# Four selective-scan layers and a routed network: new places for the matrix pieces of a step, other accumulator banks, and the head of the routed part earlier

## The reference, cut to what matters

```python
h = einsum('bhid,oi,od->bho', x, weighted_sum, weight)      # (4, 512, 256), float32
x = layernorm(h)
for _ in range(4):                                          # four layers with the same weights
    n = rmsnorm(x)
    x_in, res = split(n @ W_in, 2)                          # 256 -> 2 x 512
    u = silu(causal_conv4(x_in) + conv_b)
    dt, B, C = split(u @ W_x, [64, 80])                     # 64, 16 and 16 columns
    delta = softplus(dt @ W_dt + b_dt)
    # over the 512 positions t, for 512 channels and 16 states:
    #   h[t] = exp(delta[t] * A) * h[t-1] + delta[t] * u[t] * B[t];   y[t] = sum over states of h[t] * C[t]
    x = ((y + u * Dp) * silu(res)) @ W_out
h = h + x
z = layernorm(h)                                            # 2048 tokens of 256
e = argmax(z @ W_router)                                    # one of 4 experts for each token
y = gelu(z @ W1[e] + b1[e]) @ Wo + bo + z
out = h + layernorm(y) * gamma + beta
```

## Time and profile before

| | us |
|---|---|
| three executions | 2059.36, 2062.27, 2064.65 |
| median | 2062.27 |
| profiled execution, its own time | 2073.18 |
| profiled execution, span | 2071.5 |
| busy in the span: PE, weight loads of PE, DVE, ACT, POOL | 1850.7, 1465.2, 1564.5, 1464.7, 1538.3 |

### The profile page before, as it was taken

How to read it: one execution, slowest core, us unless ns; L and a number is a source line. 1 busy time by engine, 2 the same in 40 slices (tenths; PEclk the granted TensorE clock), 3 DMA queues, 4 the chain that set the end, 5 groups by cost and what they waited for, 6 DMA issues and landing times.

```text
span 2071.5 us, 31985 instructions
## 1 busy us (share of the span) xinstructions
PE 1850.7 (89%) x12240; PEld 1465.2 (71%) x12240; DVE 1564.5 (76%) x1703; ACT 1464.7 (71%) x2467; POOL 1538.3 (74%) x896
## 2 busy tenths in 40 slices
PE   6989899999999999999999999999898986779994
PEld 3447677777777777777777777777677775669893
DVE  1358989798989897979798988888888887752232
ACT  0268888888888888888878787878797884613231
POOL 0039898889898988888888888888989896750331
PEclk9989999999999999999999999999999998899997
DMA  7211111111111111110111111111111112152542
GB/s 248 101 51 43 52 43 61 43 62 43 62 43 62 43 61 43 48 55 34 62 41 63 41 63 42 63 41 63 42 63 41 53 52 72 62 178 85 226 144 91
DMA packets 46394, 144.27 MB, mean 70 GB/s; under 512 B 7009, under 2 KB 18529, under 8 KB 42914
## 3 DMA queue, kind: packets, MB, share of 16 engines
...
## 4 chain that ended last, share of the span: by engine, by line
PE 52%; DVE 19%; issue 12%; ACT 12%; POOL 2%; DMA 2%; SPq 0%; DVEq 0%; POOLq 0%; ACTq 0%
PE b_ps L1316 12%; DVE hid L1043 10%; PE y_all L1327 9%; ACT dub_t L694 6%; ACT hid L681 5%; DVE u L851 4%; PE bank_b L1199 3%; PE bank_a L1449 3%; PE y_all L1118 3%; PE bank_b L1214 3%; PE bank_a L1223 3%; PE b_ps L1434 2%; PE y_all L1434 2%; PE bank_a L1247 2%; PE bank_a L1214 2%
## 5 line engine op out<-in xcount | busy, mean ns | idle before, releaser
L1043 DVE TENSOR_TENSOR_SCAN hid<-hid,b_ps 128x512 f32<-128x512 f32 x1024 | 1218.3, 1210 | 243.2 <-PE b_ps L1316 222.8
L504 POOL TENSOR_TENSOR hid<-hid,c_rep 128x1024 f32<-128x1024 f32 x512 | 1210.3, 2383 | 221.5 <-DVE hid L1043 221.5
L1316 PEld LDWEIGHTS b_ps<-ident,dub_t 128*128 128x128 f32 x4096 | 488.7, 143 | 375.5 <-issue 231.1
L1316 PE MATMUL b_ps<-ident,dub_t 128*128 128x128 f32 x4096 | 634.9, 278 | 78.9 <-DVE hid L1043 74.9
L681 ACT ACTIVATE hid<-delta,neg_a 128x512 f32<-128x512 f32 x1024 | 652.7, 710 | 0.2
L1327 PE MATMUL y_all<-ident,hid 128*128 128x128 f32 x4096 | 620.6, 275 | 3.8 <-POOL hid L504 3.8
L694 ACT ACTIVATE dub_t<-du_t,b_t 128x512 f32<-128x512 f32 x768 | 490.2, 711 | 54.8 <-PE b_ps L1316 53.1
L1327 PEld LDWEIGHTS y_all<-ident,hid 128*128 128x128 f32 x4096 | 485.7, 143 | 4.8 <-POOL hid L504 4.8
L495 POOL TENSOR_SCALAR dub_t<-du_t,b_t 128x512 f32<-128x512 f32 x256 | 173.8, 707 | 0.0
L1199 PE MATMUL bank_b<-xn,w_in_sb 128*128 128x512 f32 x256 | 134.5, 612 | 15.6 <-DVE xn L838 12.5
L851 DVE SCALAR_TENSOR_TENSOR u<-bank_b,conv_w_sb,u 128x511 f32<-128x511 f32 (+2 forms) x192 | 139.4, 726 | 0.7
...
## 6 DMA issues: line engine op xcount, KB each, us to landing
c_rep<-bc_dram SPq DMA_DIRECT2D x128, 512.0 KB, 3.6
...
z_dram<-du SPq DMA_DIRECT2D x2, 1408.0 KB, 18.9
...
```

What stands on the lines that cost most here:

```text
L504: nc.gpsimd.tensor_tensor(part, part, c_rep[:, n % 2, s % GROUP, :].unsqueeze(1) .broadcast_to([P, HALF, SEQ]), ALU.mult).then_inc(hc_read ...
L1043: nc.vector.tensor_tensor_scan(hid[:, i % RING, d, :], hid[:, i % RING, d, :], b_ps[d % 2][:, :], 0.0, ALU.mult, ALU.add)\
L1316: last = nc.tensor.transpose(b_ps[d % 2][:, c * P:(c + 1) * P], dub_t[:, i % DUB, c, d * P:(d + 1) * P], ident[:, :])
```

## The change

**The tables.** Every table of places has new numbers, and is now keyed by the piece; a place with s of 16 or more lies in the next step. `squares` moves from (5, 3) to (6, 0) and from `bank_a` to `bank_b`, `b_turn` from (6, 0) to (6, 3), `spread_norm` from (8, 2) to (8, 3). The backs stand at (4, 3), (6, 0), (8, 3), (9, 0) and were at (4, 2), (5, 1), (8, 0), (8, 3); the second of them now uses `bank_a`. The taps of a block no longer stand in four slots in a row. Each piece has its own wait for its bank, where some waited for more than that.

**B turned.** `b_turn` is four full transposes, and `b_copy` reads the 16 columns out of each 128.

**ACT.** A function `between` puts copies, exponentials, logarithms and gates also in the middle of a state's four decays or four products. The four gates of a step are in two pairs within state 4, (1, 0) and (2, 3), so that four table loads stand there where two stood.

**POOL.** `POOL_B` is (4, 7, 9, 13) and was (6, 7, 10, 12); in step 15 ACT makes the products with B of all states. `times_u` and `root` move by half a state.

**Head and dispatch.** Batch 0's head stands in step 14 (states 9 to 15) and its choice early in step 15; batch 1's in states 4 to 9 of step 15; `rank(0)` and `lay_out(0)` in states 10 and 11. POOL issues the first W1 load after the half (11, 1), the eight `send_z(0)` in states 12 and 13, and the second and third W1 load in states 14 and 15.

**The tail.** The first tile follows directly on the last sums; `last_back`, `last_out` and the head of batches 2 and 3 stand among tiles 0 to 6. W1 loads 7 to 11 come before `send_z(1)`. There are 12 turns of tiles in place of 11, since tiles 10 and 21 stand alone. SP's `load_z(0)` comes ahead of a store and a load of x.

```diff
+TURNS = [tuple(range(t, min(t + 2, TILES))) for t in range(0, TILES, 2)]
+TURNS += [tuple(t + TILES for t in turn) for turn in TURNS]
+TURN_OF = {t: p for p, turn in enumerate(TURNS) for t in turn}
...
-POOL_B = (6, 7, 10, 12)
+POOL_B = (4, 7, 9, 13)
...
+            r_bank = (bank_a, bank_b, bank_a, bank_b)
+            dt_bank = (bank_a, bank_b, bank_a, bank_b)
+            back_bank = (bank_b, bank_a, bank_a, bank_a)
+            out_bank = (bank_a, bank_a)
+            x_bank = (bank_b, bank_b, bank_b, bank_b)
...
+def act_b(k):
+    return tuple(range(STATE)) if k == STEPS - 1 else ACT_B
...
+    LOAD_W1_AT = {(11, 1): 0, (14, 0): 1, (15, 0): 2}
+    SEND_Z_AT = {(12, 0): (0, 1), (12, 1): (2, 3), (13, 0): (4, 5), (13, 1): (6, 7)}
...
-                if live(k + 1) and (s, half) == (6, 1):
+                if live(k + 1) and (s, half) == (7, 0):
                     times_u(k + 1, 0)
-                if live(k + 1) and (s, half) == (7, 1):
+                if live(k + 1) and (s, half) == (8, 0):
                     times_u(k + 1, 1)
-                if live(k + 2) and (s, half) == (5, 1):
+                if live(k + 2) and (s, half) == (6, 0):
                     root(k + 2)
-                if live(k) and half == 1 and s + 3 in POOL_B:
+                if inner(k) and half == 1 and s + 3 in POOL_B:
                     times_b(k, s + 3)
-                if k == STEPS - 1 and (s, half) == (3, 0):
+                if (k, s, half) == (STEPS - 2, 11, 1):
                     head_root(0)
-                if k == STEPS - 1 and (s, half) == (10, 1):
+                if (k, s, half) == (STEPS - 1, 6, 0):
                     head_root(1)
...
+            if d == HALF:
+                between(k, s, 1)
...
+            if tc == HALF and s:
+                between(k, s - 1, 3)
...
+    def between(k, s, part):
+        at = (s, part)
+        if at == (1, 3) and live(k - 2):
+            x_copy(k - 2, 1)
+        if at == (4, 1) and live(k + 1):
+            nc.scalar.preload_act_table(ACT.Silu)
+            gate(k + 1, 1)
+            gate(k + 1, 0)
+            for m in range(NI):
+                silu(k + 1, m)
+            nc.scalar.preload_act_table_set("natural_log_exp_and_others")
+        if at == (4, 3) and live(k + 1):
+            nc.scalar.preload_act_table(ACT.Silu)
+            gate(k + 1, 2)
+            gate(k + 1, 3)
+            nc.scalar.preload_act_table_set("natural_log_exp_and_others")
...
+        if at == (7, 2) and live(k + 1):
+            delta_exp(k + 1, 0)
+            delta_log(k + 1, 0)
+        if at == (7, 4) and live(k + 1):
+            delta_exp(k + 1, 1)
+        if at == (8, 0) and live(k + 1):
+            delta_log(k + 1, 1)
...
-    TAP_AT = {(9, 2): (0, 0), (9, 3): (0, 1), (10, 0): (0, 2), (10, 1): (0, 3),
...
+    TAP_AT = {(0, 0): (9, 2), (0, 1): (10, 1), (0, 2): (10, 2), (0, 3): (10, 3),
...
-    JOIN_AT = {(1, 0): (0, 0), (2, 1): (0, 1), (9, 0): (1, 0), (9, 3): (1, 1)}
...
-                last = nc.tensor.matmul(bank_a[:, t:t + 1], xn[:, c, t * P:(t + 1) * P],
+                last = nc.tensor.matmul(bank_b[:, t:t + 1], xn[:, c, t * P:(t + 1) * P],
...
-            if tc == 0 and k >= 3:
-                pe.wait_ge(x_out_ready, DC * (k - 2))
-            if tc == 0 and 1 <= k < 3:
-                pe.wait_ge(du_t_ready, TC * k)
-            if tc == 1:
-                pe.wait_ge(conv[NI - 1], CONV * (k + 1))
-            if tc >= 2:
-                pe.wait_ge(gate_ready, TC * k + tc - 1)
...
-        pe.wait_ge(gate_ready, TC * (k + 1))
-        if k >= 2:
-            pe.wait_ge(y_ready, NI * (k - 2) + 2)
+        if live(k + 1):
+            pe.wait_ge(ss_ready, k + 2)
+        else:
+            pe.wait_ge(y_ready, NI * (k - 2) + 1)
         for c in range(TC):
-            last = nc.tensor.matmul(bank_b[:, c * STATE:(c + 1) * STATE], dbl[:, c * P:(c + 1) * P],
-                                    ident[:, RANK:RANK + STATE], start=True, stop=True)
+            last = nc.tensor.transpose(bank_b[:, c * P:(c + 1) * P], dbl[:, c * P:(c + 1) * P], ident[:, :])
         last.then_inc(bt_done, 1)
...
+    def back_bank_free(k, dc):
+        if dc == 0:
+            if live(k + 2):
+                pe.wait_ge(gate_ready, TC * (k + 2) + 4)
+            else:
+                pe.wait_ge(delta_ready, NI * (k + 1) + 4)
+        elif dc == 1:
+            if live(k + 2):
+                pe.wait_ge(dbl_ready, k + 3)
+            else:
+                pe.wait_ge(x_out_ready, DC * (k - 1) + 2)
+        elif dc == 2:
+            if live(k + 2):
+                pe.wait_ge(delta_ready, NI * (k + 2) + 3)
+            else:
+                pe.wait_ge(y_ready, NI * k + 2)
+        elif dc == 3:
+            pe.wait_ge(y_ready, NI * k + 3)
...
-    R_AT = {(0, 3): (1, 0), (1, 0): (1, 1), (1, 1): (0, 0), (1, 2): (0, 1),
-            (3, 0): (2, 0), (3, 1): (2, 1), (3, 2): (3, 0), (3, 3): (3, 1)}
...
-    BACK_AT = {(4, 2): 0, (5, 1): 1, (8, 0): 2, (8, 3): 3}
+    R_AT = {(0, 0): (0, 2), (0, 1): (1, 2), (1, 0): (1, 0), (1, 1): (1, 1), (3, 0): (2, 3), (3, 1): (3, 2),
+            (2, 0): (3, 0), (2, 1): (4, 0)}
...
+    BACK_AT = {0: (4, 3), 1: (6, 0), 2: (8, 3), 3: (9, 0)}
...
+    SQUARES_AT, B_TURN_AT, SPREAD_AT = (6, 0), (6, 3), (8, 3)
...
-    H_TURN_AT = {(0, 2): (0, 0), (1, 2): (0, 1), (8, 2): (1, 0), (9, 2): (1, 1)}
...
-    for dc in range(NI):
-        last_back(dc)
-    h_turn(2, 0)
-    h_turn(2, 1)
-    last_out(0)
-    last_out(1)
     tile_turn(0)
     expert(0)
+    last_back(0)
+    last_back(1)
     for t in range(ALL_TILES):
-        if t % 2 == 0 and t + 2 < ALL_TILES:
-            tile_turn(t // 2 + 1)
+        if t in (turn[0] for turn in TURNS) and TURN_OF[t] + 1 < len(TURNS):
+            tile_turn(TURN_OF[t] + 1)
+        if t == 5:
+            z_turn(3, 1)
         if t + 1 < ALL_TILES:
             expert(t + 1)
-        if t in (0, 2):
-            z_turn(2 + t // 2, 0)
-            z_turn(2 + t // 2, 1)
-        if t in (1, 3):
-            logits(2 + t // 2)
+        if t == 0:
+            last_back(2)
+            last_back(3)
+        if t == 1:
+            last_out(0)
+            last_out(1)
+        if t == 2:
+            h_turn(2, 0)
+            h_turn(2, 1)
+        if t == 3:
+            z_turn(2, 0)
+            z_turn(2, 1)
         if t == 4:
+            logits(2)
+            z_turn(3, 0)
+        if t == 5:
+            logits(3)
+        if t == 6:
             rank(1)
         project_out(t)
         mam.close()
```

603 lines of the change are left out of this document (340 added, 263 removed), and 6 rows, old and new, of the table TAP_AT.

## The result

| | before | after |
|---|---|---|
| median | 2062.2 us | 1902.5 us (1898.95 to 1903.89, 4 runs) |
| profiled execution, its own time | 2073.2 | 1902.3 |
| its span | 2071.5 | 1900.6 |
| busy PE, DVE, ACT, POOL | 89, 76, 71, 74% | 95, 81, 79, 80% |

What follows compares the result with a forecast made beforehand. PE and DVE, coupled by the two buffers of b_ps, were taken as bound by places of work, not busy time. Terms -106 - 6 - 2 - 52 + 6 = -160 us against the median 2062.27 gave 1902, range 1865 to 1968.

Steps and rivals of the forecast that it cites:

- Steps 1 to 13: The 13 inner steps: a step goes from 105.2 to 97.0 us, -106 in all; bounds -35 more and +52.
- The walk: Count of PE's and DVE's pieces through the 64 slots of a step: 101.8 us before, 94.3 after.
- I take 1 us a step, so the shortfall stays 2.7: Inner steps: 1 us allowed for ACT, and 2.7 us added to the slot count of 94.3, giving 97.0.
- The wait of `back` 2: States 4 to 8: its 1.76 us wait for the third softplus goes, 1.3 of the 2.7 us shortfall.
- the 2.5 us of lead: State 4: ACT's 15.2 us of work, met two states ahead, leaves it 2.5 us ahead of PE.
- Rival B: Steps: ACT, POOL and DVE hold each other through hid, dub_t and gates; step 101.5 to 102, total 1965 us; chance 0.18.
- Rival D: State 4: ACT comes without its lead and PE stops; step 112.2 us, total 2105; chance 0.04.
- The parts costed at nothing: New bank waits, half-state moves of times_u and root, and the stretch ahead of step 0: no cost or change.
- Step 14: Step 14 with batch 0's head added: from 94.5 to 92.5 us, -2; bounds 89 and 98.
- Step 15: Step 15 to first tile: half (11, 1) near 72 us, two paths ending together, 109 in all, -52; bounds 98 and 125.
- The tiles: Tiles: 12.5 us of added work less 6.1 gone from expert 8's wait and slow run, +6.
- Rival E: POOL's indirect DMAs, 11 now beside scans, last longer there: 12 us on POOL's path, total 1914; chance 0.05.

Runs made afterwards that it cites:

- The two runs made from the kernel before: Only the taps spread as in the change, 2063.8 us; only B's turn as four full transposes, 2048.5 us; each against the kernel before.

## Why the prediction was right, point by point

**Steps 1 to 13: the mechanism right, the size short.** The walk gave 22.8, 30.8 and 40.7 us for the three groups of states; the trace has 22.9, 30.8 and 41.1. What was mis-sized is the step "I take 1 us a step, so the shortfall stays 2.7": it is 0.6. (By its own terms, 2.7 less 1.3 and 1 more, it should have been 2.4 and the steps -110.) The wait of `back` 2 went as forecast, the clock is full in every step, and PE has no wait for ACT; DVE's scans wait 1.4 us a step for decays. ACT waits 2.2 us for `gating` ahead of its first gate (a wait for the buffer of the gates), so that it has time in hand there; the 2.5 us of lead were not used up. 13 x 2.1 are the 28 us.

**Rival B** (three engines over 88 us in 97 hold each other) is refuted as a sum of busy times, and its mechanism is real at single places. ACT was busy for 89.4 of 94.8 us, and the step is 94.86; a late pair of decays costs 1.2 us a step and the old choice of states 3.9 (the runs with two loads and with the old `POOL_B`). The forecast costed `POOL_B` on POOL alone; of the parts that were tried one by one it is the most mis-sized. The walk has no ACT in it, and by it neither edit should have moved the step. **Rival D** did not happen: PE has no wait on a gate in the 13 steps.

**The parts costed at nothing**: the bank waits cost nothing. Of the 4.0 us of PE's waits 3.3 are `du_turn` behind POOL's `du`, 0.25 a step; the forecast had the move of `times_u` at nothing. The stretch ahead of step 0 did not stay the same: 5.2 us less, with B's turn and the clock (that edit alone took 3.7 there in the kernel before) and other places.

**Step 14** failed by 7 us at "it gains batch 0's head, two turns, 13 DVE instructions and a root" for nothing: one of these instructions lasted 5.33 us beside POOL, and behind its idle 6.66 us PE ran at half clock until 1539.7. Taking the instruction away (the addition on POOL) brought the step only from 99.65 to 98.7, since the next one met POOL's run. **Step 15** failed at "twelve states of 6.0": 92.4 us to the half (11, 1), not 72. Of the 20 us, five instructions of DVE that waited for POOL have 9 (1.84, 0.73, 1.98, 2.37 and 2.12; 1.1 of it would be theirs with POOL idle). I put the rest down to the head's own instructions between scans and to PE at a granted clock of 0.87; how it divides was not tried. Behind the half the forecast had 37 us and the trace has 38.0. But the two paths that it called equal are not. POOL's halves set the end, and the rows were there 10.9 us before PE came to them: 5.1 us behind the last store, where the forecast took the 15 of before. Putting the whole dispatch behind the halves goes too far; a place between the two was not tried.

**The tiles**: +3.4 for +6; the first expert ran in 3.84, at full clock, where 6.30 was expected. PE had waited 0.78 us ahead of it. The +3.4 hides an error in the term. The forecast counted 6.1 us as gone, expert 8's wait of 3.26 and its slow 6.49. The two runs made from the kernel before have the old tail unchanged, and neither shows them. The window of the tiles and expert 8 in the one with the taps spread:

```profile
1865.80:2033.70 167.90, 166.94 (x1162) 156.64 (x1162) 45.04 (x109) 53.22 (x181) 36.73 (x36) 1.00 0.43 156
```

```profile
1928.48 3.81 PE L1434 MATMUL b_ps<-hid,delta 128*128 128x128 f32 x32 [0.55 <-issue]
```

In the other the tiles take 169.5 us. Against these two the tail of the change, 179.2, is 10 to 11 us longer, close to the 12.5 that the forecast had for what it adds; the gain of 6.1 came with the one execution that was profiled.

**Rival E** looked for contention between DVE and POOL at the indirect DMAs beside scans. They take 1.0 to 1.2 us there, as in the earlier trace rows. The contention was elsewhere and the other way round, DVE's small head instructions waiting for POOL's long ones. That these have 5.33 and 9 us in the two steps, near the 12 of the rival, is chance.

**The exact agreement is chance.** The sum on its own basis was 10.9 us short. The executions of the kernel before in all these runs lie between 2055 and 2073 us, and on the whole their mean clock falls as the time rises (0.979 at 2055.0, 0.972 at 2072.0). Most of the 10.9 by which the profiled one lies above the median fits its tiles, 6 to 8 us longer than in the two other traces with the same tail; its five steps with a slow stretch, 1.7 us each, are hardly unusual, since the run with the taps spread has four. How often either comes in an execution that is not profiled is not known.
